# Blank bf16 multiplications in TensorE's pauses, and a new start-up order in three attentions of head size 8

## The reference

```python
x = _layernorm(x + _L0_attn_ref(x, ...))       # 16 heads of 64, latent keys and values, causal
x = _layernorm(x + _L0_xattn_ref(x, ctx_1024, ...))   # two-way attention with a gate
x = _layernorm(x + _L0_ffn_ref(x, ...))        # two layers: local attention + GELU feed-forward
x = _layernorm(x + _L1_attn_ref(x, ...))       # Mamba scan
x = _layernorm(x + _L1_xattn_ref(x, ctx_1024, ...))   # 16 heads of 8
x = _layernorm(x + _L1_ffn_ref(x, ...))        # quantised linears, convolution, SiLU
x = _layernorm(x + _L2_attn_ref(x, ...))       # attention over the 4 entries of axis 1
x = _layernorm(x + _L2_xattn_ref(x, ctx_1024, ctx_1024, ...))   # 16 heads of 8
x = _layernorm(x + _L2_ffn_ref(x, ...))        # 8 experts and a shared one
x = _layernorm(x + _L3_attn_ref(x, ...))       # 16 heads of 8, banded mask
x = _layernorm(x + _L3_xattn_ref(x, ctx_1024, ctx_1024, mask_BxSxS2_bk1, ...))   # 16 heads of 64
x = _layernorm(x + _L3_ffn_ref(x, ...))        # 7 experts and a shared one
```

## Time and profile before

| | us |
|---|---|
| median of 3 runs | 1740.1 |
| range of the runs | 1735.97 to 1740.1 |
| the profiled execution | 1741.43 |
| its span in the profile | 1739.5 |
| PE busy | 1373.3 (79%) |
| DVE busy | 1061.4 (61%) |
| ACT busy | 708.0 (41%) |
| POOL busy | 395.8 (23%) |

### The profile page before, as it was taken

The page is one execution under the profiler, slowest core; times in us unless marked ns, Lnnn a source line. Parts: engine busy times, 40 slices in busy tenths (PEclk is TensorE's granted clock), DMA queues, the critical chain, the costliest instruction groups (busy, mean ns, idle before and its releaser), DMA issues.

```text
span 1739.5 us, 24466 instructions
## 1 busy us (share of the span) xinstructions
PE 1373.3 (79%) x8622; PEld 865.3 (50%) x8622; DVE 1061.4 (61%) x2379; ACT 708.0 (41%) x2003; POOL 395.8 (23%) x308
## 2 busy tenths in 40 slices
PE   7999757777777556755687545889979899989997
PEld 4666535554455422222354434556556566656664
DVE  2556666664676568898766777665567455553333
ACT  4554324444444354544245411452224455532222
POOL 1333013222332033445630013310010133320000
PEclk9999878998889757667889776899979999989999
DMA  8000000000000310000000000000000000000000
GB/s 336 1 1 1 1 0 1 0 0 1 1 1 0 134 62 0 0 0 0 1 2 1 1 0 1 1 2 1 0 1 2 1 1 1 1 1 1 0 0 13
DMA packets 4204, 24.81 MB, mean 14 GB/s; under 512 B 1168, under 2 KB 3216, under 8 KB 3472
## 3 DMA queue, kind: packets, MB, share of 16 engines
q1 hardware_dynamic: 4112, 23.59, 3.3%
HBM read 23.06 MB, written 0.52 MB: 14 GB/s over the span
## 4 chain that ended last, share of the span: by engine, by line
PE 58%; DVE 18%; issue 15%; POOL 4%; ACT 4%; DMA 1%; DVEq 0%; POOLq 0%; SPq 0%; ACTq 0%
PE PS L628 5%; PE PS L1053 5%; PE PS L1038 4%; PE PS L1039 4%; PE PS L312 4%; PE PS L344 3%; PE PS L324 3%; PE PS L696 3%; PE PS L285 2%; DVE arena L2074 2%; PE PS L293 2%; PE PS L353 2%; POOL arena L2702 2%; PE PS L306 2%; PE PS L287 2%
## 5 line engine op out<-in xcount | busy, mean ns | idle before, releaser
L536 POOL TENSOR_TENSOR arena<-arena,small 128x768 f32<-128x768 f32 (+1 forms) x64 | 107.8, 1684 | 228.4 <-DVE small L479 117.3
L866 DVE TENSOR_REDUCE arena<-PS 128x2 f32<-128x512 f32 (+1 forms) x192 | 108.5, 609 | 66.8 <-PE PS L622 66.1
L793 ACT ACTIVATE arena<-PS 128x512 f32<-128x512 f32 (+1 forms) x192 | 92.2, 532 | 120.0 <-PE PS L628 120.0
L1142 DVE TENSOR_TENSOR arena<-arena,PS 128x512 f32<-128x512 f32 x82 | 56.4, 688 | 116.3 <-ACT arena L1075 116.2
L2130 POOL TENSOR_TENSOR arena<-arena 128x512 f32<-128x512 f32 x64 | 103.9, 1644 | 92.0 <-DVE arena L2056 34.0
L1075 ACT ACTIVATE arena<-PS 128x512 f32<-128x512 f32 x82 | 49.0, 597 | 166.8 <-PE PS L1039 166.8
L628 PE MATMUL PS<-arena 32*128 32x256 f32 (+1 forms) x768 | 102.2, 384 | 12.7 <-DVE arena L866 11.0
L416 ACT ACTIVATE arena<-PS,small 128x256 f32<-128x256 f32 (+1 forms) x256 | 110.8, 453 | 0.0
L2065 DVE TENSOR_TENSOR_SCAN arena<-arena 128x512 f32<-128x512 f32 x64 | 94.0, 1473 | 23.2 <-ACT arena L1963 15.8
L622 PE MATMUL PS<-arena 32*128 32x256 f32 (+1 forms) x768 | 103.3, 398 | 4.4 <-DVE arena L866 4.4
L1868 PE MATMUL PS<-arena,w_consts 128*128 128x512 f32 x128 | 92.3, 818 | 4.3 <-DVE arena L2074 4.3
(11 more groups left out here) (410 smaller groups left out, 3167.0 us busy)
## 6 DMA issues: line engine op xcount, KB each, us to landing
w_last<-in_last SPq DMA_DIRECT2D x1, 8260.0 KB, 22.2
w_rest<-in_rest SPq DMA_DIRECT2D x1, 5898.5 KB, 36.8
w_last<-in_first SPq DMA_DIRECT2D x1, 4532.5 KB, 21.2
w_last<-in_first SPq DMA_DIRECT2D x1, 2176.0 KB, 10.2
X<-in_x SPq DMA_DIRECT2D x1, 512.0 KB, 4.4
CT<-in_ctxT SPq DMA_DIRECT2D x1, 512.0 KB, 10.9
out<-X SPq DMA_DIRECT2D x1, 512.0 KB, 3.2
w_consts<-in_consts SPq DMA_DIRECT2D x1, 373.0 KB, 3.1
```

The lines of the kernel that those rows point to most:

```text
L536: g.tensor_tensor(p, p, ri, ALU.mult).then_inc(self.pn_done.sem, 1)
L866: v.tensor_reduce(dst, src, AX.X, ALU.max, negate=True).then_inc(self.mx_done.sem, 1)
```

## The change

`keep_warm` issues n multiplications of the bf16 identity with a tile of zeros, 512 columns each, into a bank of `PS` that nobody reads at that place. They have no wait of their own, so PE issues them as soon as its queue comes to them. They are put:

- at each layer end, 14 (or 5 where only two tiles are left) before the transposes, and 4 after them;
- in `BitLinear`, 24 before the wait for the weights and 4 per iteration;
- in `TwoWay`, 8 per iteration before the wait for `y_ready`;
- in `LocalLayer`, 3 + 8 + 2 per iteration, before the waits for `x1_ready`, `n_ready` and `n_ev`.

In all 329 are executed. `NarrowAttention` gets other first steps on PE and DVE: `by_key` of pairs 0 and 1 joins `score` of pairs 3 and 4, the value projections move back by one step each, and DVE's shifts and copies change places with maxima.

```diff
+def keep_warm(c, pe, bank, n):
+    for _ in range(n):
+        pe.matmul(c.PS[:, bank, :], c.IDB[:, :], c.blank[:, :], start=True, stop=True, skip_group_check=True)
...
     def tensor(self, pe):
         if not self.last:
+            keep_warm(self.c, pe, self.spare, 5 if len(self.groups) == 2 else 14)
             self.transposes(pe, len(self.groups) - 1)
+            keep_warm(self.c, pe, 3, 4)
...
-                if k == 1:
-                    pe.wait_ge(self.v_ev.sem, self.v_ev.at(0, 1))
...
-        values_of(0, 5)
         block(None, 2)
-        maxima(0)
         pe.wait_ge(self.k_ev.sem, self.k_ev.at(0, 2))
         pe.wait_ge(self.q_ev.sem, self.q_ev.at(0, 2))
+        values_of(0, 6)
+        maxima(0)
+        block(0, 3)
+        block(1, 4)
+        pe.wait_ge(self.v_ev.sem, self.v_ev.at(0, 1))
         values_of(2, 6)
-        block(None, 3)
-        block(0, None)
-        block(None, 4)
         maxima(1)
-        for i in range(4 * B):
+        block(None, 5)
+        block(None, 6)
+        maxima(2)
+        for i in range(1, 4 * B):
             b, r = divmod(i, 4)
-            if i == 0:
-                block(None, 5)
-            else:
-                block(2 * i, 2 * i + 5 if i + 2 < 4 * B else None)
-                values(i - 1)
+            block(2 * i, 2 * i + 5 if i + 2 < 4 * B else None)
+            values(i - 1)
             block(2 * i + 1, 2 * i + 6 if i + 3 < 4 * B else None)
...
-        for q in range(4):
+        for q in range(5):
             maxima(q)
-        values_of(0, 5)
+        shift(0)
         if self.band is not None:
             biased(2)
-        shift(0)
-        values_of(2, 6)
+        for q in range(5, 8):
+            maxima(q)
+        values_of(0, 6)
+        for q in range(8, 10):
+            maxima(q)
+        shift(1)
         if self.band is not None:
             biased(3)
-        for q in range(4, 10):
+        values_of(2, 6)
+        for q in range(10, 14):
             maxima(q)
-        shift(1)
+        shift(2)
...
@@ BitLinear.tensor @@
+        keep_warm(c, pe, 3, 24)
         pe.wait_ge(self.w_ready.sem, self.w_ready.at(0, 1))
...
+            keep_warm(c, pe, 6, 4)
             for t in range(2):
                 pe.wait_ge(self.hq_ready.sem, self.hq_ready.at(it, t + 1))
...
@@ TwoWay.tensor @@
+            pe.wait_ge(self.z_ready.sem, self.z_ready.at(it, 0))
+            keep_warm(c, pe, 5, 8)
             pe.wait_ge(self.y_ready.sem, self.y_ready.at(it, 1))
...
@@ LocalLayer.tensor @@
+            keep_warm(c, pe, 4, 3)
             pe.wait_ge(self.x1_ready.sem, self.x1_ready.at(it, 1))
...
+            keep_warm(c, pe, 4, 8)
             pe.wait_ge(self.n_ready.sem, self.n_ready.at(it, 1))
...
+            keep_warm(c, pe, 4, 2)
             pe.wait_ge(self.n_ev.sem, self.n_ev.at(it, 1))
```

More of the change, by code:

```diff
@@ L108, in __init__ @@
         self.IDB = sb("IDB", [P, P], BF16)
+        self.blank = sb("blank", [P, 512], BF16)
         self.arena = sb("arena", [P, 17600])
@@ L137, with __init__ @@
 class LayerEnd:
-    def __init__(self, c, z_ready, last=False, early=False, counted=0, reload=False):
+    def __init__(self, c, z_ready, last=False, early=False, counted=0, reload=False, spare=3):
+        self.spare = spare
         self.c, self.z_ready, self.last, self.reload = c, z_ready, last, reload
@@ L907, in vector @@
         v.wait_ge(self.cleared.sem, self.cleared.at(0, 3))
-        for q in range(4):
+        for q in range(5):
             maxima(q)
-        values_of(0, 5)
+        shift(0)
         if self.band is not None:
             biased(2)
-        shift(0)
-        values_of(2, 6)
+        for q in range(5, 8):
[4 more added lines that the diff above has]
+        shift(1)
         if self.band is not None:
             biased(3)
-        for q in range(4, 10):
+        values_of(2, 6)
+        for q in range(10, 14):
             maxima(q)
-        shift(1)
+        shift(2)
+        if self.band is not None:
+            biased(4)
         if self.bo is not None:
             v.wait_ge(self.xb_ready.sem, self.xb_ready.at(0, 1))
-        for i in range(4 * B):
+        for i in range(1, 4 * B):
             b, r = divmod(i, 4)
@@ L2916, in build @@
                              counted=s.ITERS if isinstance(s, Experts) else 0,
-                             reload=isinstance(s, (Mamba, BitLinear, Experts)))
+                             reload=isinstance(s, (Mamba, BitLinear, Experts)), spare=2 if isinstance(s, Mamba) else 3)
             c.arena_free = (s.z_ready, s.z_ready.last)
@@ L2961, in _ @@
             v.wait_ge(loaded["consts"], 16)
+            v.memset(c.blank[:, :], 0.0)
             v.tensor_copy(c.IDB[:, :], c.ident)
```

## The result

The changed kernel takes 1718.3 us (median of 4 runs, 1709.49 to 1718.9), the kernel before 1739.55 (4 runs, 1735.97 to 1740.1): a ratio of 0.987, 95% interval 0.9836 to 0.9905. Its profiled execution took 1718.44 us. The forecast was 1717. So the sum came out right, and in part by luck: `again`, the same kernel on another chip, has a median of 1713.6. The terms did not come out: the layer ends brought more than the prediction said, the new order less, and the loops nothing together.

A forecast was written before the change was run, and what follows sets the result against it. PE, holding 58% of the chain, was taken to bound the kernel in places, its clock falling in pauses. Terms 10 + 3 + 3 + 11.4 - 3 - 1 = 23.4 us off 1741.43 gave 1718, as a median 1717; range 1703 to 1736.

The forecast's parts named there:

- blanks do not raise the clock: Rival, all blanks: products with zeros might not count as load; 1734 us, or 1737 with cold blanks; chance 0.06.
- Layer ends, +10: Blanks at layer ends let later stages start at full clock: 10 us gained, 45% of a 22.1 us ceiling.
- Part of the cold work is also hidden: Stage starts: in the attentions ACT and DVE alternate with PE, a reason for taking 45% of the ceiling, 10 us.
- transposes let the clock fall: Rival, layer ends: lightly loaded transposes don't hold the clock, nine starts stay cold, 10 us missing: 1727; chance 0.19.
- The order, +11.4: NarrowAttention's new first steps cut DVE's waits before the 17th maximum in L1x, L2x and L3a: 11.4 us gained together.
- The walk: NarrowAttention's new order timed step by step from the first maximum: the 17th after 17.5 us, where L1x took 22.9.
- the new order moves its waits: Rival, NarrowAttention: values wait for DVE's later copy, so only a quarter of 11.4 us comes: 1726; chance 0.08.
- TwoWay, +3: 8 blanks per iteration fill one of TwoWay's two pauses and warm the work behind: 3 us gained, bounds 0 and 7.8.
- L1473 should take 2.0 us in most iterations: Sign of success in TwoWay: this product takes 2.0 us at a warm clock, where it took 3.58.
- I take 3, as one of the two pauses stays: TwoWay's second pause, 1.75 us without blanks, can still lower the clock, so 3 us is taken of at most 7.8.
- BitLinear, +3: Blanks at BitLinear's start and in its iterations: 1 us at the start and 0.7 in each of 3 iterations, 3 gained.
- LocalLayer, -3: Three blanks on LocalLayer's path cost 0.64 us in each of 6 iterations, 3.9, less 1 us gained: net 3 lost.

The follow-up runs named there:

- light_blanks: The changed kernel with all 329 blanks cut from 512 columns to 8: 1730.99 us, ratio 0.9956 to the kernel before.
- ends_only: The changed kernel with blanks at the layer ends alone, none in BitLinear, TwoWay and LocalLayer: 1716.12 us, ratio 0.9871 to the kernel before.
- order_only: The changed kernel with NarrowAttention's new first steps but no blank anywhere: 1731.1 us, ratio 0.9956 to the kernel before.
- ends_more: The changed kernel with 18 blanks for 14 before eight-tile transposes and a 256-column blank behind each of the first seven: 1710.14 us.
- blanks_only: The changed kernel with all its blanks, but NarrowAttention's first steps as before: 1721.29 us, ratio 0.9906 to the kernel before.
- best_nolocal: As best, but also without the 8 and 2 blanks of LocalLayer: 1708.23 us, ratio 0.9824 to the kernel before.
- best: The changed kernel with the edits of ends_more, local_no3 and twoway_6 together: 1702.42 us, ratio 0.9798 to the kernel before.
- twoway_6: The changed kernel with 6 more blanks in TwoWay's second pause, behind the transposes of Y: 1709.63 us, ratio 0.9836 to the kernel before.
- local_no3: The changed kernel without the 3 blanks ahead of the transposes of X1 in LocalLayer: 1708.63 us, ratio 0.9831 to the kernel before.

## Why the prediction was right, and where it wasn't

**The mechanism** (load in the pauses keeps TensorE's clock up): right on average, though not place by place. light_blanks shows that load does it, and the rival "blanks do not raise the clock" is excluded: 0.878 and 1731 us with light ones, 0.912 and 1718 with full ones.

**Layer ends, +10:** undersized, 15 us measured. I took 45% of the 22.1 us that the nine starts could give, since I expected part of the cold work to be hidden. I followed the rows of DVE and ACT one by one. In the first 12 us of the nine stages ends_only gets ahead of order_only by some 15 us in all and of light_blanks by 12.5, which is 68% and 57% of that ceiling. It gets ahead most at the starts that are wholly warm. These are two of the nine windows before:

```profile
246.60:252.50 5.90, 5.88 (x7) 2.48 (x8) 4.64 (x15) 0.99 (x2) 2.89 (x4) 0.50 0.00 0
...
1367.70:1372.10 4.40, 4.40 (x11) 3.52 (x12) 0.39 (x1) 1.29 (x4) 2.59 (x1) 0.51 0.00 2
```

Half of them is 2.95 us in L0f and 2.2 in L3x; the gain is 2.9 to 3.1 and 2.4. The step that failed is "Part of the cold work is also hidden": where a start stays warm, none of it is. The ceiling was too low as well, since I had read only the starts. L2x and L3a gain 1.2 and 1.4 us more from 20 us on, where PE was cold a second time. Here is L3a in order_only, and then about the same work in ends_only:

```profile
1286.60:1290.00 3.40, 3.40 (x38) 1.95 (x37) 2.35 (x7) 0.89 (x3) 0.00 (x0) 0.51 0.00 0
```
```profile
1274.00:1277.40 3.40, 3.40 (x58) 2.13 (x56) 2.42 (x8) 1.23 (x4) 0.00 (x0) 1.00 0.00 0
```

Not all of the gain is sure to be the blanks'. L1x is 2.8 us shorter in ends_only than in order_only, but as long as in light_blanks (92.62 and 92.54).

**The rival "transposes let the clock fall"** holds at some ends. In the changed kernel three starts are wholly warm of those shown, and with more load before and between the transposes the ends of L1f and L2f are warm as well. By the Trainium skill (TensorE: Matmul & The Clock Gate, Part 4, PE-mode transpose) transposes don't count as busy for the clock gate in the way matmuls do. Those two ends agree with it but don't show it: ends_more also has four more blanks in front, and no run here has the one without the other. The rival's time (1727) did not come, since with 14 blanks in front and 4 behind the eight transposes L0f and L1x start warm. Which of the blanks did that wasn't tried.

**The order, +11.4:** oversized, 7.5 us alone. The walk itself was good. In L1x the first shift ended 4.8 us after the start of the first maximum (walked: 4.6), the second copy ended at 10.6 (10.5), the third shift at 14.2 (13.8). Only the last steps were later, 18.4 in place of 17.5. In L2x and L3a order_only needs 19.6 and 17.7: its walks gain 4.5 + 1.7 + 3.3 = 9.5 us of the 11.4, and its stages 7.4. What the walk took for granted was the full clock. In ends_only, whose L1x and L3a stand at 0.98 where order_only has 0.93 and 0.91, the 17th maximum comes at 16.8, 18.4 and 16.3 us, 13.7 less than before in all. The mean clock alone doesn't tell: L1x of the changed kernel has 0.98 too and still needs 18.4 us, because its one cold stretch (0.50 from 870.8 to 874.1) lies ahead of the 17th maximum. In the changed kernel the three walks gain 4.5, 2.9 and 4.7 us (the 17th maximum comes at 18.4, 18.4 and 16.3), 12.1 in all. But 2.9 of these come in blanks_only too, so 9.2 are the order's, and 8.7 of its stages. The step that failed is that I booked a walk at the full clock as the order's alone. The rival "the new order moves its waits" is out: in the first 23 us behind the first maximum of L1x no wait of PE names DVE's copy of values (L864).

**TwoWay, +3:** not there in the first profile (L0x 66.59 against 66.84), and there in `again` (61.92). I had written that one of the two pauses stays; what stayed with it was a cold stretch, and it lay on L1489, for which ACT's L1547 waits. "L1473 should take 2.0 us in most iterations" was wrong in one execution and right in another. The term isn't a fixed number. The mis-sized step is "I take 3, as one of the two pauses stays": with the eight blanks alone 12 of 18 turns are cold, with six more in the pause that stayed none of 9.

**BitLinear, +3:** 1.85 us against ends_only. The 1 us at the start came, but not as I had it. The transposes start 957.18 - 948.24 = 8.94 us after the small matmul, as before (966.23 - 957.29), not near 8, because DVE sets that time. They run warm instead, 1.09 us in place of 1.97, and by 18 us into the stage DVE is 1.2 us ahead. The iterations failed: the second weight's product takes 2.01 us in three of four, yet only 0.7 us of that comes through, where I had 2.1.

**LocalLayer, -3:** the mechanism and price were right to 0.01 us per iteration (0.64 predicted, 0.65 measured), and its total too (3.9; L0f is 4.2 us shorter without the three). Wrong was "the same idle time of 0.83 behind it on DVE": it is 1.47, since DVE isn't delayed and PE is. And the other ten blanks gain 3.2 us between best_nolocal and best, not 1. They lose 0.6 in the first depth, gain 1.2 at the turn of the depths, to which I had put the 1 us, and gain 2.6 behind it, 2.3 of them in the last iteration, which I had left out. Over the stage the changed kernel is 3.6 us shorter than before, not longer, since its warm start counts too.

So the total was right by errors that cancel, which is luck: +6 at the ends (15 where I had 10 less the 1 for late blanks), -4 in the order, -1 in BitLinear, -3 in TwoWay and +2 in LocalLayer (whose blanks cost 1.2 us between ends_only and the changed kernel, where I had said 3).

## What to carry to other kernels

Here blank multiplications paid at the turn of stages, where a pause of PE is followed by dense work that others wait for: 15 us there, and nothing clear from those in the loops together. Price them by their columns, and put none ahead of a PE instruction that already starts without idle time. Look for every pause near the cold work: in TwoWay the eight blanks in one of two pauses left most turns cold. And run a kernel several times and compare stages, not only totals: the same kernel without any edit moved by half a per cent.

## What was unexpected of the hardware

The granted clock doesn't fall and rise at fixed places of the program. Beside each other on one chip, 9 runs of the kernel before lie within 6.1 us (1735.62 to 1741.71) and 5 of the changed kernel spread over 9.6. The product L1489 at the first turn takes 3.40 us in one execution of the changed kernel and 1.99 in another, and the start of L0x is warm in best and cold in best_nolocal, 0.06 us apart and with the same code up to there. L1a, a scan stage that PE doesn't bound, is 254.4 to 254.7 us long in six kernels' profiles and 256.5 to 257.2 in the other seven, the kernel before among these; `again` and the changed kernel, which are the same, stand on either side. What ties L1a's length to this wasn't tried. It also stays open how much of the gains of twoway_6 and local_no3 over the changed kernel comes from their edit: 3.9 us for the three local blanks are sure, 0.65 in each of 6 iterations, while L0x took 60.3 us in twoway_6, 61.2 in best, and 61.9 in `again` without the six.
